# A token encoder with linear attention and routed experts: normalising undivided heads, copying the doubled payload columns on ScalarE, and moving one down product and one image's places

## The chip, the cores and the metric

The kernel runs on 1 core of one Trainium2 chip. The metric is the device time of one execution in microseconds; lower is better. The engines are TensorE (PE, matmuls), VectorE (DVE), ScalarE (ACT), GpSimd (POOL) and the DMA queues, among them SyncE's (SP). Each engine takes its own instructions strictly in the order in which they were written, and waits on semaphores for the others.

## The reference

Four images of 512 tokens, model width 192. Every token first gets a Fourier feature projection; then one layer of gated linear attention and one layer of routed and shared experts follow, each with a residual. Cut to what matters here:

```python
h = einsum('bnf,of->bno', concat([sin(xb), cos(xb)]), W)      # xb = 2*pi*x*freq, 6912 features
h = concat([cls_tok, h], axis=1)
# attention, x = layernorm(h)
numerator   = einsum('blm,blmd->bld', q, Mstate)
denominator = einsum('blm,blm->bl', q, z)[..., None] + 1e-06
heads  = numerator / denominator
normed = (heads - mean(heads)) / sqrt(var(heads) + 1e-05) * gamma + beta
h = h + normed @ Wo
# experts, x = layernorm(h)
top-2 of 8 experts by softmax(x @ router_w), gates normalised to sum 1
routed = sum_e gate_e * (silu(x @ w_gate_e) * (x @ w_up_e)) @ w_down_e
shared = (silu(x @ ws_gate) * (x @ ws_up)) @ ws_down
h = h + alpha * shared + (1 - alpha) * routed                   # alpha = sigmoid(x @ sg_w + sg_b)
```

## The kernel before

The order of every engine's work is written out by hand. Attention runs for five sequences a: a = 0 is the class token (2 rows, the same for all images), a = 1 to 4 (B = 4) are the images with four tiles of 128 tokens. The program has three stretches.

**Token stretch.** For each image b, `project(b, k)` for k = 0 to 8 multiplies the sine and cosine features of nine blocks (L1369, 48 matmul instructions a block as the profile counts them). The features come from POOL (L426), DVE (`remainders`, L801 and L805) and ACT (`sines`, L511 and L514). The attention of the image before is woven between the blocks on every engine: `attn0(a)` ... `attn8(a)`. For a = 0 this runs inside image 0's own nine blocks.

**Shared stretch.** After the last block, PE runs 24 chunks q (6 for each image) of the shared expert: `up(q)` (two products of five matmuls, L1533 to L1537), with `down(q - 2)` (L1571) behind it. ACT makes `silu(q)` (L616), DVE `hidden(q)` (L1077). `up(q)` waits for `hidden(q - 2)`, `down(q)` for `hidden(q)`, and the first `down` of an image waits for `finish` of the image before (L1085, semaphore `out_ready`), which empties its PSUM banks. 19 chunks (NQB) run here, and the attention of image 4 (a = B) is woven in by a table of chunk numbers: `Q_LN2` = 6 (its heads), `Q_X2` = 7, `Q_LN3` = 9 (third layernorm), `Q_X3` = 10 (transposes), `Q_LG` = 11, `Q_RK` = 12 (router, gates, ranks).

**Tile stretch.** Tokens are scattered by expert into `slots` in HBM, from two copies of the payload (`pay_a`, `pay_b`), by POOL's indirect DMAs (L456), which wait for the positions that `places(a, [1])` writes (L1053). SP then loads `xs` from `slots` (L386) in groups of 1, 2, 4, 5, ... tiles, and 39 tiles run through `tile_x`, `tile_up`, `tile_hidden_t` and `tile_down`. The last five shared chunks and the combination follow.

Steps that the change touches:

- `attn5(a)` on DVE: `divide` adds 1e-6 to the denominators (L900), takes reciprocals (L904) and writes the divided heads from PSUM into `xn` (L908); `norm_heads` then runs `layernorm` on `xn`: bn_stats (L771), bn_aggr (L774), twelve steps of Newton's inverse square root on four numbers a row (L778 to L784), and the final subtract and multiply (L787).
- `layernorm(..., twice=True)` in `attn7(a)`: the payload has 256 columns, of which the last 64 repeat columns 128 to 192 (for the high and low parts of a product). DVE writes them with an instruction of its own for each tile (L790). PE's `attn8(a)` transposes columns 0 to 128 (L1491) and 128 to 256 (L1493); POOL's `second_payload` copies the payload (L441).
- `places(B, ...)`: three pieces of small DVE steps that turn ranks into positions.
- `down(NQB - 1)`: the down product of chunk 18, the first of image 4, in the tile loop; it waits for `finish(2)`, which DVE runs behind `tile_low(0)`.

## Time and profile before

| | us |
|---|---|
| median of 3 runs | 556.94 |
| lowest, highest | 554.76, 557.33 |
| the profiled execution's own time | 554.62 |
| its span, first to last instruction | 552.8 |
| PE busy in it | 535.8 |
| DVE busy | 370.3 |
| ACT busy | 244.4 |
| POOL busy | 180.3 |

The span is cut by what PE does: about 6 to 350 us is the token stretch, 352 to 443 us the shared stretch, 443 to 525 us the tiles, and the rest is the tail. The granted TensorE clock is full in all slices.

A row of the timeline reads: start in us from the span's start, length in us, engine, line, operation, output <- inputs, shape, number of merged instructions, and in brackets the engine's idle time before it with what ended it. A matmul's end is modelled: in a dense row of 0.40 us matmuls the next one starts 0.23 us after the one before, so an idle time understates the delay against a dense follower by about 0.15 us.

### The profile page before, as it was taken

What the parts mean: (1) busy time and instruction counts of PE and PEld (TensorE: products, weight loads), DVE (VectorE), ACT (ScalarE), POOL (GpSimd) and SP (SyncE); (2) the same over time, 40 slices, a digit from 0 to 9 for tenths busy, and PEclk for the clock granted to TensorE, in tenths of its full rate; (3) what the DMA queues carried; (4) which work ended last, traced back from release to release, by engine and by line L of the source; (5) the groups of instructions that cost most, each with busy time, mean ns of one, the idle gap of its engine ahead of it and who ended that gap; (6) DMA issues with size and microseconds to landing.
All of it is one profiled execution on the core that took longest, in us unless ns stands there. A gap on an engine that the chain in (4) does not pass through costs nothing.

```text
span 552.8 us, 9034 instructions
## 1 busy us (share of the span) xinstructions
PE 535.8 (97%) x3235; PEld 504.8 (91%) x3235; DVE 370.3 (67%) x1065; ACT 244.4 (44%) x343; POOL 180.3 (33%) x205
## 2 busy tenths in 40 slices
PE   5999999999999999999999999999999999999997
PEld 5998999899999899999989999978877899999865
DVE  8637787534868637978853995468998256666437
ACT  3465464755324764243565422264142135555410
POOL 6413134122234311765212460002601414444510
PEclk9999999999999999999999999999999999999999
DMA  8900067000000001110000010510103441531174
GB/s 330 341 23 20 7 219 250 20 10 20 20 19 21 20 0 27 62 59 0 1 1 10 20 59 1 185 54 30 50 0 125 157 136 47 171 99 51 52 216 142
DMA packets 23488, 42.49 MB, mean 77 GB/s; under 512 B 2502, under 2 KB 15044, under 8 KB 23348
## 3 DMA queue, kind: packets, MB, share of 16 engines
q1 hardware_dynamic: 19560, 33.31, 18.4%
q0 software_dynamic: 3472, 8.07, 4.1%
q10 hardware_dynamic: 412, 0.53, 0.4%
q8 instruction: 27, 0.44, 0.3%
q14 instruction: 17, 0.14, 0.1%
HBM read 31.74 MB, written 14.79 MB: 84 GB/s over the span
## 4 chain that ended last, share of the span: by engine, by line
PE 80%; DVE 11%; ACT 4%; issue 2%; DMA 1%; ACTq 0%; DVEq 0%
PE ps L1369 44%; PE ps L1571 3%; PE ps L1624 2%; PE ps L1626 2%; PE ps L1533 1%; PE ps L1602 1%; PE ps L1603 1%; PE ps L1604 1%; PE ps L1606 1%; PE ps L1605 1%; DMA r<-r 1%; PE ps L1537 1%; PE ps L1535 1%; PE ps L1536 1%; PE ps L1534 1%
## 5 line engine op out<-in xcount | busy, mean ns | idle before, releaser
L1369 PE MATMUL ps<-w_tok,feat 128*128 128x192 f32 x1728 | 289.4, 328 | 7.5 <-ACT feat L502 6.2
L1369 PEld LDWEIGHTS ps<-w_tok,feat 128*128 128x128 f32 x1728 | 282.9, 191 | 8.7 <-issue 8.7
L426 POOL TENSOR_SCALAR feat<-fx 128x512 int32<-128x512 f32 x108 | 93.4, 880 | 189.4 <-PE ps L1369 185.8
L511 ACT ACTIVATE feat<-feat 128x1536 f32<-128x1536 f32 x35 | 52.0, 1485 | 110.1 <-DVE feat L805 110.1
L801 DVE SCALAR_TENSOR_TENSOR feat<-fx,feat 128x512 f32<-128x512 f32 x105 | 76.5, 781 | 1.8 <-POOL feat L426 1.5
L462 POOL DMA_INDIRECT ydram<-yr,xs x39 | 37.8, 969 | 53.9 <-DVE yr L1127 53.9
L514 ACT ACTIVATE feat<-feat,half_pi 128x1536 f32<-128x1536 f32 x35 | 54.6, 1561 | 0.0
L456 POOL DMA_INDIRECT slots<-pay_a,posi x17 | 17.4, 1025 | 75.2 <-DVE posi L1053 71.8
L805 DVE TENSOR_SCALAR feat<-feat 128x1536 int32<-128x1536 int32 x35 | 37.3, 1066 | 1.2
L1571 PE MATMUL ps<-w_down,hid_ring 128*128 128x192 f32 x192 | 35.4, 328 | 2.2 <-DVE H L1085 2.2
L616 ACT ACTIVATE s_ring<-ps 128x512 f32<-128x512 f32 x24 | 14.4, 599 | 52.4 <-PE ps L1537 52.4
L1571 PEld LDWEIGHTS ps<-w_down,hid_ring 128*128 128x128 f32 x192 | 31.6, 190 | 4.1 <-issue 3.1
L1077 DVE TENSOR_TENSOR hid_ring<-s_ring,ps 128x512 f32<-128x512 f32 x24 | 16.3, 684 | 18.3 <-PE ps L1537 15.3
L638 ACT ACTIVATE xhr<-ps 128x256 fp32r<-128x256 f32 x39 | 15.0, 384 | 22.1 <-PE ps L1584 22.1
L1120 DVE TENSOR_TENSOR hidt<-sr,ps 128x192 f32<-128x192 f32 x39 | 13.8, 354 | 15.8 <-ACT sr L644 15.8
L1113 DVE TENSOR_TENSOR xlr<-ps,xhr 128x256 fp32r<-128x256 f32 x39 | 16.5, 424 | 10.6 <-ACT xhr L638 10.6
L1533 PE MATMUL ps<-X,wa_hi 128*128 128x512 f32 x48 | 22.0, 458 | 0.8 <-ACT s_ring L616 0.8
L849 DVE TENSOR_TENSOR_SCAN r<-one,s_c,r 128x512 f32<-128x512 f32 x4 | 5.1, 1283 | 25.4 <-ACT r L556 25.4
L1127 DVE TENSOR_SCALAR yr<-ps,xs 128x192 f32<-128x192 f32 x39 | 16.3, 418 | 8.6 <-PE ps L1626 8.6
L644 ACT ACTIVATE sr<-ps 128x192 f32<-128x192 f32 x39 | 12.9, 330 | 20.1 <-PE ps L1606 20.1
L456 POOL DMA_INDIRECT slots<-pay_b,posi x17 | 19.0, 1120 | 5.2 <-issue 5.2
L1624 PE MATMUL ps<-wd_ea,htr 128*128 x78 | 19.2, 328 | 0.7 <-DVE yr L1127 0.7
(306 smaller groups left out, 859.6 us busy)
## 6 DMA issues: line engine op xcount, KB each, us to landing
slots<-in_blank SPq DMA_DIRECT2D x1, 5031.0 KB, 19.2
w_tok<-in_wT SPq DMA_DIRECT2D x7, 576.0 KB, 8.9
fx<-in_xT SPq DMA_DIRECT2D x15, 256.0 KB, 2.7
xs<-slots SPq DMA_DIRECT2D x5, 645.0 KB, 5.8
yin<-ydram SPq DMA_DIRECT2D x8, 384.0 KB, 6.6
raw_a<-in_wea SPq DMA_DIRECT2D x4, 384.0 KB, 5.4
raw_b<-in_web SPq DMA_DIRECT2D x4, 384.0 KB, 6.0
w_tok<-in_wT SPq DMA_DIRECT2D x4, 288.0 KB, 7.5
```

Of the source, the lines that this page charges most:

```text
L426: ins = pool.tensor_scalar(feat[:, k % SLOTS, i, :].bitcast(I32), x[:, x_block(k), :], f_col[:, fi:fi + 1], 1.0, ALU.mult, ALU.mult)
L456: pool.indirect_dma_start(slots, bass.IndirectOffsetOnAxis(ap=idx, axis=0), (pay_a[a % 2], pay_b)[c][0:TP, t, :], None).then_inc(scat, 16)
L462: pool.indirect_dma_start(ydram, bass.IndirectOffsetOnAxis(ap=idx, axis=0), yr[:, s % NYR, :], None).then_inc(yscat[s % NYR], 16)
L511: act.activation(feat[:, k % SLOTS, 0:3, :], feat[:, k % SLOTS, 0:3, :], ACT.Sin, scale=TWO_PI).then_inc(sin_ready, 1)
L514: act.activation(feat[:, k % SLOTS, 3:6, :], feat[:, k % SLOTS, 3:6, :], ACT.Sin, bias=half_pi[:, :], scale=-TWO_PI).then_inc(sin_ready, 1)
L801: ins = dve.scalar_tensor_tensor(feat[:, s, i, :], x[:, x_block(k), :], f_col[:, fi:fi + 1], feat[:, s, i, :].bitcast(I32), ALU.mult, ALU. ...
L805: dve.tensor_scalar(feat[:, s, 3:6, :].bitcast(I32), feat[:, s, 0:3, :].bitcast(I32), 0x7FFFFFFF, None, ALU.bitwise_and).then_inc(r_ready, 1)
L1113: dve.tensor_tensor(xlr[:, s % 2, :], ps[:, XT[s % 2], 0:2 * P], xhr[:, s % 2, :].bitcast(F32), ALU.subtract).then_inc(rxl_ready, 1)
L1369: ins = pe.matmul(ps[:, TOK[a % 2][t // 2], (t % 2) * D:(t % 2 + 1) * D], feat[:, k % SLOTS, i, t * P:(t + 1) * P], w_tok[:, k, i, :], sta ...
L1533: pe.matmul(o, wa_hi[:, c, i, :], xh, start=True, stop=False)
L1571: ins = pe.matmul(ps[:, DN0 + t // 2, (t % 2) * D:(t % 2 + 1) * D], hid_ring[:, q % 3, t * P:(t + 1) * P], w_down[:, c, :], start=(c == 0 ...
L1624: pe.matmul(o, htr[:, s % 2, 0:P], wd_ea[:, bass.ds(e, 1), :].rearrange("p e n -> p (e n)"), start=True, stop=False)
```

## The change

1. **Heads.** The reciprocal and the divided copy are gone. With h = s/d (d is the denominator plus 1e-6), (h - mean h) / sqrt(var h + eps) equals (s - mean s) / sqrt(var s + eps d^2) for positive d, so `layernorm` now reads the undivided sums s in PSUM, and its variance gets eps d^2 (`den2`) in place of eps. DVE's bn_stats and its last step both read PSUM.
2. **Doubled columns.** L790 is gone for all five sequences. ACT copies columns 128 to 192 to 192 to 256 in one instruction, `twice(a)`, which waits for `xn2_ready` and raises `twice_ready`. PE's second group of transposes and POOL's `second_payload` wait for `twice_ready`. For a = 0 to 3 `twice` stands ahead of ACT's `attn8(a)`, for a = 4 ahead of `silu(10)`.
3. **Places of image 4.** `places(B, [0])` goes from before to after `hidden(12)`, `places(B, [1])` from after `hidden(12)` to after `hidden(14)`.
4. **Last chunk's down product.** `down(18)` goes from the tile loop's turn 1 to turn 2, behind `tile_hidden_t(0)`.

```diff
@@ DVE, layernorm
-            def layernorm(src, dst, a, which, TP, nt, done, twice=False, parts=(0, 1, 2)):
+            def layernorm(src, dst, a, which, TP, nt, done, over=None, parts=(0, 1, 2)):
...
                     for i in range(nt):
-                        ins = dve.bn_stats(st[0:TP, i, :], src[0:TP, i, 0:D])
+                        ins = dve.bn_stats(st[0:TP, i, :], src(i))
+                    if over is not None:
+                        for lo, d in over:
+                            n = d.shape[1]
+                            ins = dve.tensor_scalar(den[0:TP, lo:lo + n], d, DEN_EPS, None, ALU.add)
                     next_(ins)
                     for i in range(nt):
                         ins = dve.bn_aggr(mv[0:TP, i, :], st[0:TP, i, :])
+                    if over is not None:
+                        ins = dve.scalar_tensor_tensor(den2[0:TP, 0:nt], den[0:TP, 0:nt], LN_EPS, den[0:TP, 0:nt],
+                                                       ALU.mult, ALU.mult)
...
-                    next_(dve.tensor_scalar(v_, mv[0:TP, 0:nt, 1], LN_EPS, None, ALU.add))
+                    if over is None:
+                        next_(dve.tensor_scalar(v_, mv[0:TP, 0:nt, 1], LN_EPS, None, ALU.add))
+                    else:
+                        next_(dve.tensor_tensor(v_, mv[0:TP, 0:nt, 1], den2[0:TP, 0:nt], ALU.add))
...
-                        if twice:
-                            ins = dve.tensor_scalar(dst[0:TP, i, D:XD], src[0:TP, i, P:D], mv[0:TP, i, 0:1],
-                                                    y[0:TP, i:i + 1], ALU.subtract, ALU.mult)
@@ DVE, attn5
-            def divide(a):
...
-                dve.reciprocal(rden[0:TP, 0:nt], den[0:TP, 0:nt]).then_inc(rden_ready, 1)
...
-                    ins = dve.tensor_scalar(xn_[0:TP, i, 0:D], ps[0:TP, AV_BANK[i // 2], c0:c0 + D],
-                                            rden[0:TP, i:i + 1], None, ALU.mult)
...
+                layernorm(heads, normed(a), a, 1, TP, nt, hn_ready, over=sums)
@@ ACT
+            def twice(a):
+
+                act.wait_ge(xn2_ready, a + 1)
+                act.activation(payload(a)[:, :, D:XD], payload(a)[:, :, P:D], ACT.Copy).then_inc(twice_ready, 1)
+
             def attn8(a):
...
+                if a < B:
+                    twice(a)
                 act.wait_ge(xpose3, a + 1)
...
+                if q == Q_X3:
+                    twice(B)
                 silu(q)
@@ POOL, second_payload
-                pool.wait_ge(xn2_ready, a + 1)
+                pool.wait_ge(twice_ready, a + 1)
@@ DVE, main order
                     gates(B)
-                    places(B, [0])
...
                 hidden(q)
...
                 if q == Q_RK:
+                    places(B, [0])
+                if q == Q_RK + 2:
                     places(B, [1])
-                if q == Q_RK + 2:
                     places(B, [2])
@@ PE, attn8
+                pe.wait_ge(twice_ready, a + 1)
                 for i in range(nt):
                     ins = pe.transpose(ps[:, A1, i * P:(i + 1) * P], pay_[:, i, P:XD], ident)
@@ PE, tile loop
-                if i == 1:
-                    down(NQB - 1)
                 if 2 <= i < NTILE + 2:
                     tile_hidden_t(i - 2)
+                if i == 2:
+                    down(NQB - 1)
```

PE's order at the end of the class token's attention (a = 0, between blocks 6 and 7 of image 0), before:

```order
L1369 MATMUL ps<-w_tok,feat 128x192 x11
L1369 MATMUL ps<-w_tok,feat 128x192 [waits sin_ready]
L1369 MATMUL ps<-w_tok,feat 128x192 x11
L1491 MATMUL ps<-pack,pay_a 128x128 [waits xn2_ready]
L1493 MATMUL ps<-pack,pay_a 128x128
L1369 MATMUL ps<-w_tok,feat 128x192 [waits sin_ready,wt_in7]
```

and with the change:

```order
L1374 MATMUL ps<-w_tok,feat 128x192 x11
L1496 MATMUL ps<-pack,pay_a 128x128 [waits xn2_ready]
L1499 MATMUL ps<-pack,pay_a 128x128 [waits twice_ready]
L1374 MATMUL ps<-w_tok,feat 128x192 [waits sin_ready,wt_in7]
L1374 MATMUL ps<-w_tok,feat 128x192 x11
```

Nothing moved, but the second transpose got a wait. What that wait is for stands on ACT; its order at the same place with the change (L511 and L514 are `sines(0, 7)`, L593 is `twice(0)`, L603 and L604 `attn8(0)`):

```order
L511 ACTIVATE feat<-feat 128x1536 [waits r_ready]
L514 ACTIVATE feat<-feat,half_pi 128x1536
L593 ACTIVATE pay_a<-pay_a 2x64 [waits xn2_ready]
L603 ACTIVATE xc<-ps 128x2 [waits xpose3]
L604 ACTIVATE xc<-ps 128x2
L511 ACTIVATE feat<-feat 128x1536 [waits r_ready]
```

The copy is new, and stands behind both sine instructions of block 7.

DVE's order over chunks 12 to 14, before (L1030 to L1041 are `places(B, [0])`, L1043 to L1055 `places(B, [1])`, L1059 begins `places(B, [2])`):

```order
L1011 TENSOR_TENSOR pay_b<-p,om 128x4
L1030 TENSOR_TENSOR aft<-cnt,rks 128x8 [waits rk_ready]
...
L1041 SCALAR_TENSOR_TENSOR dd<-gap,dold 128x8 [waits pos_step]
L1077 TENSOR_TENSOR hid_ring<-s_ring,ps 128x512 [waits silu_ready,down_ready,u_psum,pos_step]
L1043 TENSOR_TENSOR slot<-rks,base 128x32
...
L1053 CAST posi<-posf 128x8 [waits scat,pos_step]
L1055 COPY cnt<-aft 128x8
L1077 TENSOR_TENSOR hid_ring<-s_ring,ps 128x512 [waits silu_ready,down_ready,u_psum,pos_step]
L1085 SCALAR_TENSOR_TENSOR H<-ps,alpha,H 128x192 [waits down_ready]
L1085 SCALAR_TENSOR_TENSOR H<-ps,alpha,H 128x192 x3
L1077 TENSOR_TENSOR hid_ring<-s_ring,ps 128x512 [waits down_ready,silu_ready,u_psum]
L1059 COPY nbk<-nba 128x8
```

and with the change:

```order
L1017 TENSOR_TENSOR pay_b<-p,om 128x4
L1083 TENSOR_TENSOR hid_ring<-s_ring,ps 128x512 [waits down_ready,silu_ready,u_psum]
L1036 TENSOR_TENSOR aft<-cnt,rks 128x8 [waits rk_ready]
...
L1047 SCALAR_TENSOR_TENSOR dd<-gap,dold 128x8 [waits pos_step]
L1083 TENSOR_TENSOR hid_ring<-s_ring,ps 128x512 [waits silu_ready,down_ready,u_psum,pos_step]
L1091 SCALAR_TENSOR_TENSOR H<-ps,alpha,H 128x192 [waits down_ready]
L1091 SCALAR_TENSOR_TENSOR H<-ps,alpha,H 128x192 x3
L1083 TENSOR_TENSOR hid_ring<-s_ring,ps 128x512 [waits down_ready,silu_ready,u_psum]
L1049 TENSOR_TENSOR slot<-rks,base 128x32
...
L1059 CAST posi<-posf 128x8 [waits scat,pos_step]
L1061 COPY cnt<-aft 128x8
L1065 COPY nbk<-nba 128x8 [waits pos_step]
```

`finish(1)` (L1085, now L1091) now stands ahead of the piece that writes the positions `posi`.

## Rows read from the trace of the kernel before

**Rows 1.** The page: busy time (us), share of the span, instructions, by engine.

```profile
PE 535.8 (97%) x3235; PEld 504.8 (91%) x3235; DVE 370.3 (67%) x1065; ACT 244.4 (44%) x343; POOL 180.3 (33%) x205
```

**Rows 2.** Waits of PE: line <- what it waited for: us in total, times, longest.

```profile
PE ps L1571 <- DVE H L1085: 2.2, 3, 1.1
```

**Rows 3.** Timeline of PE at the class token's last transposes.

```profile
68.73 0.27 PE L1493 MATMUL ps<-pack,pay_a 128*128 128x128 f32 x1
69.20 8.04 PE L1369 MATMUL ps<-w_tok,feat 128*128 128x192 f32 x48 [0.20 <-ACT feat L511]
```

**Rows 4.** Timeline of ACT there.

```profile
67.56 1.49 ACT L511 ACTIVATE feat<-feat 128x1536 f32<-128x1536 f32 x1 [6.57 <-DVE feat L805]
68.95 1.56 ACT L514 ACTIVATE feat<-feat,half_pi 128x1536 f32<-128x1536 f32 x1
70.42 0.15 ACT L596 ACTIVATE xc<-ps 128x2 fp32r<-128x2 f32 x1
```

**Rows 5.** Timeline of ACT at the same place of image 3.

```profile
342.62 0.60 ACT L596 ACTIVATE X<-ps 128x512 fp32r<-128x512 f32 x1 [7.88 <-PE ps L1493]
```

**Rows 6.** Timeline of DVE, heads of image 4 and what follows.

```profile
384.35 1.39 DVE L908 TENSOR_SCALAR xn<-ps,rden 128x192 f32<-128x192 f32 x4
...
394.03 3.69 DVE L1106 TENSOR_TENSOR e_b<-raw_b,e_b 64x384 fp32r<-64x384 f32 x2
```

**Rows 7.** Timeline of POOL there.

```profile
391.96 4.86 POOL L477 TENSOR_TENSOR e_lo<-raw_a,e_hi 128x384 fp32r<-128x384 f32 x5
```

**Rows 8.** Timeline of PE, shared stretch.

```profile
391.34 0.66 PE L1466 MATMUL ps<-pack,xn 128*128 128x128 f32 x4 [0.55 <-DVE xn L787]
...
399.29 1.54 PE L1571 MATMUL ps<-w_down,hid_ring 128*128 128x192 f32 x8 [0.61 <-DVE H L1085]
...
407.58 0.66 PE L1491 MATMUL ps<-pack,pay_a 128*128 128x128 f32 x4 [0.80 <-DVE pay_a L790]
...
412.36 0.24 PE L1505 MATMUL ps<-wra_hi,X 128*128 128x10 f32 x1
```

**Rows 9.** Timeline of DVE at the end of the third layernorm of image 4.

```profile
407.22 0.31 DVE L790 TENSOR_SCALAR pay_a<-H,mv,y 128x64 f32<-128x64 f32 x1
407.44 1.28 DVE L1077 TENSOR_TENSOR hid_ring<-s_ring,ps 128x512 f32<-128x512 f32 x2
```

**Rows 10.** Timeline of ACT: `silu(10)` and `silu(12)`.

```profile
405.65 0.60 ACT L616 ACTIVATE s_ring<-ps 128x512 f32<-128x512 f32 x1 [2.21 <-PE ps L1537]
...
419.91 0.60 ACT L616 ACTIVATE s_ring<-ps 128x512 f32<-128x512 f32 x1
```

**Rows 11.** Timeline of DVE: places of image 4 around `hidden(12)`.

```profile
420.64 0.17 DVE L1030 TENSOR_TENSOR aft<-cnt,rks 128x8 f32<-128x8 f32 x1 [0.97 <-ACT rks L609]
...
422.68 0.69 DVE L1077 TENSOR_TENSOR hid_ring<-s_ring,ps 128x512 f32<-128x512 f32 x1
423.29 0.18 DVE L1043 TENSOR_TENSOR slot<-rks,base 128x32 f32<-128x32 f32 x1
```

**Rows 12.** Timeline of PE: end of `up(14)`, then `down(12)`.

```profile
425.62 0.40 PE L1537 MATMUL ps<-X,wb 128*128 128x512 f32 x1
427.11 1.54 PE L1571 MATMUL ps<-w_down,hid_ring 128*128 128x192 f32 x8 [1.10 <-DVE H L1085]
```

**Rows 13.** Timeline of POOL: the first scatter of image 4.

```profile
425.66 1.00 POOL L456 DMA_INDIRECT slots<-pay_a,posi  x1 [16.77 <-DVE posi L1053]
```

**Rows 14.** Timeline of SP's queue: the first six loads of `xs`.

```profile
437.16 3.02 SPq L386 DMA_DIRECT2D xs<-slots  x6
```

**Rows 15.** DMA issues: count, KB each, median us to landing; here the first tile.

```profile
xs<-slots SPq DMA_DIRECT2D x1, 129.0 KB, 2.0
```

**Rows 16.** Timeline of PE: first tile, and `down(18)`.

```profile
443.00 0.27 PE L1583 MATMUL ps<-pack,xs 128*128 128x128 f32 x1
...
446.26 1.54 PE L1571 MATMUL ps<-w_down,hid_ring 128*128 128x192 f32 x8 [0.47 <-DVE H L1085]
```

**Rows 17.** Timeline of DVE in the first tiles: `tile_low(1)`, right behind `finish(2)`.

```profile
446.03 0.41 DVE L1113 TENSOR_TENSOR xlr<-ps,xhr 128x256 fp32r<-128x256 f32 x1
```

44 lines of the change are left out of this document (17 added, 27 removed).

## The prediction

> **What bounds the kernel now.** I read the page's busy table first: PE is busy 97% of the span, DVE 67%, ACT 44% [rows 1]. Work saved on DVE or ACT is worth nothing in itself. It counts only where PE waits, so the next view is PE's waits. The largest class in the part that the change touches is PE waiting for `finish` in front of a `down`, 2.2 us in three waits [rows 2]. Then I went through PE's timeline for every idle time in brackets, and asked of each what the waited-for engine had been doing. Outside the first 7 us and the tail, the waits within reach of the change are 0.55 us before the transposes of the heads, 0.61 before `down(6)`, 0.80 before the payload's transposes [rows 8], 1.10 before `down(12)` [rows 12] and 0.47 before `down(18)` [rows 16], all on DVE and all in the shared stretch or just behind it. In the token stretch PE has nearly no wait to give back, so there the change can only cost: what has to be looked for is a wait that it adds on a PE that is dense. Times below are positions in the old trace, and gains or losses are of PE against it.
>
> **1. The class token's `twice(0)`: a loss of 1.4 us.** PE's second transpose for a = 0 ran at 68.73, and block 7 followed at 69.20 after 0.20 us of idleness, when `sines(0, 7)` had finished its first half [rows 3]. Now that transpose waits for `twice(0)`, and `twice(0)` stands on ACT behind both halves of `sines(0, 7)`. These started at 67.56 and 68.95, and the next instruction, `attn8(0)`, started at 70.42 [rows 4]. Queued behind the waiting transpose is all of PE's block 7. One L790 less on DVE ahead of it brings the sines forward by its pitch, 407.44 - 407.22 = 0.22 us [rows 9]: `twice(0)` starts at 70.20. The trace has no ACT copy of 2x64; it lasts at least the 0.15 us of the 128x2 copy in [rows 4], and at most the 0.60 of a 128x512 [rows 5]; I take 0.24, near the small one. Then 0.04 for the semaphore, transpose at 70.48, block 7 some 0.12 later at 70.60, against 69.20: **+1.40**, between +1.3 and +1.75. From there PE is dense to image 4 and everything else in the token stretch follows PE, so nothing gives it back.
>
> For a = 1 to 3 the same wait costs nothing. ACT had sat idle for 7.88 us before image 3's `attn8` [rows 5] and longer in image 1, so it takes the copy as soon as DVE is done, while PE is still in block 7. The shorter heads and layernorms on DVE in these images are hidden under the blocks.
>
> **2. Heads of image 4: gained, then given back, 0.** The removed copy took 1.39 us [rows 6], the reciprocal and its wait some 0.2 more. Against that stand `den2`, two small operations that now share a group with others, and bn_stats from PSUM instead of SBUF. No row has bn_stats from PSUM; its bounds are its present 1.14 for four and the 1.39 that the copy from PSUM took for four, so at most 0.25 more. DVE is done at least 1.2 us sooner. PE was late by 0.55 plus the 0.15 of a modelled end, 0.7 us, so this wait goes. But DVE's next long step is not its own: L1106 (`expert_lo(0)` and `(1)`) started at 394.03 and the pair took 3.69 us, though POOL's e_lo subtractions ran to 391.96 + 4.86 = 396.82 and DVE only came through behind them [rows 6, 7]. POOL began those when its scatter of image 3 was out, which the change doesn't move. So DVE reaches L1106 at about 393.3 and leaves it at 397.7 as before; `finish(0)` and PE's `down(6)` at 399.29 stay where they are, and the wait there grows from 0.61 to about 1.3. Net **0**.
>
> The Trainium skill (SBUF — State Buffer, "SBUF: two separate sides") says that the port pair is locked for one instruction, by whichever engine starts first. By that, DVE would get in at the first boundary between POOL's five, near 393.9, and not behind the fifth; the trace of before speaks against it, since DVE came at 394.03 and passed two such boundaries unserved. What the rule would give is rival B.
>
> **3. Payload of image 4: 0.4 us.** Without four L790, less the one pitch each that they took (4 x 0.22), the last layernorm ends at 406.63 instead of 407.53, so the transposes start 0.90 sooner. `twice(4)` on ACT moves half of the 128x512 that took 0.60 [rows 5], so I take 0.4 of it; the first four transposes take 0.66 less their modelled end [rows 8], 0.5: no wait of PE, or 0.1 if the copy takes the full 0.60. But `twice(4)` stands ahead of `silu(10)`, which ran at 405.65 [rows 10] and now cannot start before 406.63 + 0.05 + 0.3 = 407.0 (0.3 being the pitch of such a copy, 0.1 under its length). Queued behind is `hidden(10)`: DVE could do it at 407.15 and gets it at 407.63, where it was at 408.04. Of the 0.90, DVE keeps 0.41. The rest of DVE's row (three `expert_lo`, the low parts of the operand) runs without a pause to PE's router at 412.36 [rows 8]. PE arrives 0.90 early and waits for DVE there: **-0.41** in all.
>
> **4. Places after `hidden(12)`: 1.3 us.** Today `places(4, [0])` starts at 420.64, `hidden(12)` at 422.68, `places(4, [1])` at 423.29 [rows 11], then `hidden(13)`, then `finish(1)`, for which PE waits 1.10 + 0.15 = 1.26 us behind the end of `up(14)` (425.62 + 0.23 = 425.85 against 427.11) [rows 12]. With the new order `hidden(12)` goes as soon as `silu(12)` is there: 419.91 + 0.60 - 0.41 = 420.10 [rows 10]. Piece 0 takes 422.68 - 420.64 = 2.04 and starts one pitch of 0.6 later, at 420.73, so `hidden(13)` stands at 422.77 and `finish(1)` runs 423.37 to 424.76. PE comes to `down(12)` at 425.85 - 0.41 - 0.04 = 425.40 and finds it done. **-1.30**; PE is now 1.71 ahead.
>
> **5. The scatter is late: 0.85 us given back.** Piece 1, which releases POOL's scatter, now stands behind `finish(1)` and `hidden(14)`. The latter needs `up(14)`: in a dense row it starts 0.44 after PE's last matmul, so 425.62 - 0.45 + 0.44 = 425.61, and piece 1 at 426.22, where it was at 423.29 [rows 11]: 2.93 us later. POOL's eight scatters, then SP's loads, then the first tile move by that: POOL 425.66 to 428.59 [rows 13], SP 437.16 to 440.09 [rows 14], landing 2.0 later [rows 15], 442.09. PE would take the first tile at 443.00 - 1.71 = 441.29 [rows 16]. It waits to about 442.15: **+0.85**. Before, the tile had landed 3.8 us ahead. The bounds are 0 (if the landing is 0.85 shorter) and 1.5 (landing at the 2.7 of the second load). Later groups have more slack, since a tile takes PE some 2 us.
>
> **6. `down(18)` a turn later: 0.** The 0.47 + 0.15 us before it [rows 16] goes. But DVE still runs `finish(2)` ahead of `tile_low(1)`, which starts 3.03 us after PE's first tile and ends at 3.44 [rows 17], and `tile_up(1)` needs it. `down(18)` covered that; without it PE arrives at 2.80 and waits 0.65. Turn 3 begins 5.98 after turn 0, against 5.95. **+0.03**, within 0.3 either way.
>
> **Sum:** 1.40 + 0 - 0.41 - 1.30 + 0.85 + 0.03 = +0.57 us. On the profiled execution's 554.62 that is 555.2. That execution lies at the low end of the three runs, 2.3 us under their median, so for the median I add it to 556.94: **557.5**. About 0.5% (2.8 us) is what a measurement of this kernel can tell from no change.
>
> **Rivals.**
> A, the steps as above, 557.5: chance 0.66.
> B, DVE slips in between POOL's subtractions: `finish(0)` would run some 2 us sooner, and PE would keep 0.7 + 0.6 + 0.9 + 0.2 = 2.4 us to the router, then 1.3 at `down(12)`; the first tile, whose scatter follows PE there, takes back about 0.8. With +1.4 from step 1 that is -1.5: 555.4. The passed boundaries speak against it. 0.08.
> C, the first tile comes in time after all, or the class token's wait is shorter than the queue says (ACT free sooner): -0.3 to -0.8, 556.4. Nothing in the rows shows a shorter landing; 0.10.
> D, slower: `twice(4)` on ACT costs DVE all that it saved, because `silu(10)` comes later than 407.3, and the places' new turn then does not free `finish(1)` in time while the scatter is late all the same. PE has +1.4, neither gain, and waits at the first tile 0.4 to 1.5 us for a landing 2.9 to 4 us late: +1.8 to +3, 559.3. It decides from the point where `hidden(12)` is more than 1 us later than I place it. Against it: `silu(12)` has no other work ahead of it than before. 0.09.
> E, that it does not do what it says: PE's doubled transposes for images 1 to 3 wait too, because `twice` stands behind `sines(b, 8)`. That costs up to 1.4 us an image, +4.8: 561.7. ACT's idle 7.88 us speaks plainly against it. 0.02. The remaining 0.05 is for medians of three that fall apart more than the steps: those before differ by 2.6 us.
>
> **Range.** The likeliest case with the bounds of steps 1, 5 and 6 spans 556.5 to 558.8; the spread of a median and cases B, C and part of D widen it to 555.0 to 559.6. Faster by over 0.5% (below 554.2) needs B and more: 0.04. Slower by over 0.5% (above 559.7) is half of D, and E: 0.07. Within: 0.89.
>
> **What the profile would show.** Step 1: PE idle about 1.5 us before the class token's second transpose, with ACT's small copy as its releaser, right behind L514. Step 2: no wait before the heads' transposes, a wait of about 1.3 before `down(6)`, and again one DVE instruction of some 3 to 4 us beside POOL's e_lo. Step 3: `silu(10)` right behind the copy, PE waiting 0.5 before the router. Step 4: no wait before `down(12)`. Step 5: PE waiting for a DMA before the first tile. Step 6: the wait before `down(18)` gone and one of 0.5 to 0.7 before the second tile's up product. I am wrong if PE shows no wait for the class token's copy, or if the first tile starts dense.

## The result, and the profile after

| | before | after |
|---|---|---|
| median, us | 556.98 (11 runs) | 560.05 (11 runs) |
| lowest, highest | 554.46, 557.52 | 557.33, 560.34 |
| ratio after to before, 95% interval | | 1.0053 [1.0032, 1.0075] |
| profiled execution: own time, span | 554.62, 552.8 | 560.13, 558.3 |
| mean granted TensorE clock in it | 1.000 | 0.993 |

The changed kernel is 3.1 us slower. The forecast was 557.5 with a range up to 559.6, so the result lies outside. Eight more runs of the same kernel on another chip gave 560.11 (ratio 1.0073 [1.0048, 1.0097]).

The first thing to see stands in the last row of the table: the two profiled executions did not have the same clock. Their spans differ by 5.5 us, their kernels' medians by 3.1.

**PE's waits.** In the view of PE's waits after the change (what waited, for whom, us in total, times, longest), the row of [rows 2] has shrunk from 2.2 to 1.4, and five rows are new or larger:

```profile
PE ps L1499 <- ACT pay_a L593: 1.6, 1, 1.6
PE ps L1577 <- DVE H L1091: 1.4, 1, 1.4
...
PE ps L1589 <- DMA xs<-slots: 1.0, 1, 1.0
...
PE ps L1608 <- DVE xlr L1119: 0.7, 1, 0.7
...
PE ps L1511 <- issue: 0.5, 1, 0.5
PE ps L1577 <- issue: 0.5, 1, 0.5
```

**Class token.** ACT's timeline: both sines, and right behind them the new copy. It answers to [rows 4], where the row at 70.42 followed the sines directly:

```profile
67.85 1.48 ACT L511 ACTIVATE feat<-feat 128x1536 f32<-128x1536 f32 x1 [6.35 <-DVE feat L825]
69.24 1.56 ACT L514 ACTIVATE feat<-feat,half_pi 128x1536 f32<-128x1536 f32 x1
70.70 0.24 ACT L593 ACTIVATE pay_a<-pay_a 2x64 f32<-2x64 f32 x1
```

PE's timeline in the same place, against 68.73 and 69.20 in [rows 3]:

```profile
71.00 0.33 PE L1499 MATMUL ps<-pack,pay_a 128*128 128x128 f32 x1 [1.58 <-ACT pay_a L593]
71.16 0.34 PE L1374 MATMUL ps<-w_tok,feat 128*128 128x192 f32 x1
```

Block 7 starts 1.96 later, and from its third matmul on the difference is 1.90. PE was already 0.52 late ahead of it, so this place costs 1.38. The 0.52 is from the first 12 us, where the kernels are the same: PE's matmuls there start 0.32 us apart at first and 0.16 apart later, and the step from one to the other comes at about 10.7 us before and 11.6 us after. In the other profiles of this document this early difference against before lies between -0.5 and +0.8 us, whatever the kernel.

**Heads, `down(6)`, `down(12)`, first tile.** PE's timeline at the places of [rows 8], [rows 12] and [rows 16]. The wait before the heads' transposes (395.75) is gone, the one before `down(6)` has grown from 0.61 to 1.40, the payload's (411.82) is gone, the router (417.12) waits 0.54, `down(12)` (430.62) waits no more, and three waits stand in the first tile turns, 0.97, 0.47 and 0.70:

```profile
395.75 0.49 PE L1471 MATMUL ps<-pack,xn 128*128 128x128 f32 x3
...
404.41 0.56 PE L1577 MATMUL ps<-w_down,hid_ring 128*128 128x192 f32 x2 [1.40 <-DVE H L1091]
...
411.82 0.66 PE L1496 MATMUL ps<-pack,pay_a 128*128 128x128 f32 x4
...
417.12 0.24 PE L1511 MATMUL ps<-wra_hi,X 128*128 128x10 f32 x1 [0.54 <-issue]
...
430.62 0.65 PE L1577 MATMUL ps<-w_down,hid_ring 128*128 128x192 f32 x3
...
447.56 0.30 PE L1589 MATMUL ps<-pack,xs 128*128 128x128 f32 x1 [0.97 <-DMA xs<-slots]
447.70 0.27 PE L1590 MATMUL ps<-pack,xs 128*128 128x128 f32 x1
448.44 0.42 PE L1577 MATMUL ps<-w_down,hid_ring 128*128 128x192 f32 x1 [0.47 <-issue]
...
452.02 0.44 PE L1608 MATMUL ps<-e_hi,xhr 128*128 x1 [0.70 <-DVE xlr L1119]
...
454.51 0.27 PE L1589 MATMUL ps<-pack,xs 128*128 128x128 f32 x1
```

The first tile (447.56) now waits for its landing, where before it started dense at 443.00 [rows 16].

**The clock.** The view by windows gives, for each stretch, the busy time and instruction count of PE, PEld, DVE, ACT and POOL, then the granted clock. Two stretches of 3.4 us in the middle of dense work ran at 0.50, that is at 1.2 GHz instead of 2.4:

```profile
182.00:185.60 3.60, 3.60 (x33) 3.60 (x31) 2.82 (x7) 2.05 (x2) 2.74 (x3) 1.00 0.00 0
185.70:189.00 3.30, 3.30 (x13) 3.30 (x12) 2.99 (x14) 3.25 (x5) 0.00 (x0) 0.50 0.00 0
...
353.60:356.30 2.70, 2.70 (x25) 2.66 (x24) 1.34 (x7) 2.16 (x3) 0.00 (x0) 1.00 0.48 113
356.40:359.70 3.30, 3.30 (x10) 2.53 (x9) 2.85 (x17) 0.60 (x1) 0.00 (x0) 0.50 0.96 299
```

PE was busy without a gap ahead of either (3.60 of 3.60 us and 2.70 of 2.70). What it did there was the row of 20 small router matmuls of an image (10 columns each): image 1's ahead of the first stretch, image 3's ahead of the second. PE's timeline shows the end of such a row and then the shared expert's products, which stand 0.43 us apart where they are 0.23 apart at full clock:

```profile
355.86 0.25 PE L1515 MATMUL ps<-wrb,X 128*128 128x10 f32 x1
355.97 0.48 PE L1539 MATMUL ps<-X,wa_hi 128*128 128x512 f32 x1
...
357.51 0.63 PE L1543 MATMUL ps<-X,wb 128*128 128x512 f32 x1
357.94 0.63 PE L1539 MATMUL ps<-X,wa_hi 128*128 128x512 f32 x1
```

PE's starts against those of before move by 1.68 us over the first stretch and by 1.55 over the second. So the 5.5 us between the two spans are 0.5 from the start, 3.2 from two half-clock stretches and 1.8 from waits. The forecast had 0.57 for the waits and nothing for the clock.

### The profile page after: what moved, and what is told of

Same layout as the page of the kernel before. It is cut to its first block, busy times and chain, and to the rows that moved or that the text cites. A ratio compares the mean times of both kernels' runs of the same rounds, so it can differ in the third digit from the quotient of the medians.

```text
span 558.3 us, 9004 instructions
## 1 busy us (share of the span) xinstructions
PE 539.3 (97%) x3235; PEld 508.0 (91%) x3235; DVE 361.9 (65%) x1031; ACT 246.0 (44%) x348; POOL 176.4 (32%) x205
## 4 chain that ended last, share of the span: by engine, by line
PE 82%; DVE 7%; ACT 4%; issue 2%; DMA 2%; POOL 1%; ACTq 0%; DVEq 0%; POOLq 0%
PE ps L1374 44%; PE ps L1577 3%; PE ps L1630 2%; PE ps L1632 2%; PE ps L1539 2%; PE ps L1541 1%; PE ps L1542 1%; PE ps L1540 1%; PE ps L1543 1%; PE ps L1608 1%; POOL slots L456 1%; PE ps L1610 1%; PE ps L1609 1%; PE ps L1612 1%; PE ps L1611 1%
## 5 line engine op out<-in xcount | busy, mean ns | idle before, releaser
L426 POOL TENSOR_SCALAR feat<-fx 128x512 int32<-128x512 f32 x108 | 88.4, 833 | 196.1 <-PE ps L1374 192.3
L511 ACT ACTIVATE feat<-feat 128x1536 f32<-128x1536 f32 x35 | 51.9, 1484 | 104.8 <-DVE feat L825 104.7
L514 ACT ACTIVATE feat<-feat,half_pi 128x1536 f32<-128x1536 f32 x35 | 54.6, 1561 | 0.0
```

What stands on the lines that cost most here:

```text
L426: ins = pool.tensor_scalar(feat[:, k % SLOTS, i, :].bitcast(I32), x[:, x_block(k), :], f_col[:, fi:fi + 1], 1.0, ALU.mult, ALU.mult)
L511: act.activation(feat[:, k % SLOTS, 0:3, :], feat[:, k % SLOTS, 0:3, :], ACT.Sin, scale=TWO_PI).then_inc(sin_ready, 1)
L514: act.activation(feat[:, k % SLOTS, 3:6, :], feat[:, k % SLOTS, 3:6, :], ACT.Sin, bias=half_pi[:, :], scale=-TWO_PI).then_inc(sin_ready, 1)
```

## The experiments

Every run's mean granted clock is listed with its time, and the times of one kernel fall into groups by it. The kernel before, in 112 runs beside these experiments: 48 runs at 1.0 of 554.4 to 555.3, 64 below it of 556.7 to 560.6. "Full-clock runs" below are those at 1.0. Because the share of them differs from kernel to kernel, a median mixes waits and clock; the full-clock runs and the trace tell the waits apart. The diffs show the lines that decide; declarations of semaphores and waits that only follow from them are left out.

**1. The changed kernel with the class token's columns back on DVE**, written by `layernorm` for a = 0 again.

```diff
@@ ACT, attn8
-                if a < B:
+                if 0 < a < B:
                     twice(a)
@@ PE, attn8
-                pe.wait_ge(twice_ready, a + 1)
+                if a >= 1:
+                    pe.wait_ge(twice_ready, a)
```

> The changed kernel, with the class token's doubled columns written by VectorE again (its ScalarE copy and TensorE's wait for it gone); all else as changed. Theory W (waits): TensorE loses 1.40 us at this wait, and nothing later gives it back, so this kernel is 1.4 us faster than the changed one, 1.0 to 1.8, near 558.6, and its trace has no wait at the class token's second transpose. Rival C (clock): most of the 3 us comes from stretches at half the TensorE clock that the changed kernel's 1.6 us stall brings on; then the stall's removal takes those stretches away too, in profile and times, and the gain is 2.5 us or more. Rival H (hidden): the next stages are not paced by TensorE and absorb it, gain under 0.5 us.

Measured: 558.05 (555.0 to 561.36, 12 runs), ratio 1.0030 [1.0010, 1.0050]. The profiled execution was at full clock, with a span of 553.2 against 552.8 before, and PE's shift is -0.04 up to `down(6)`, -0.93 at the payload, -0.41 at the router, -1.67 at `down(12)`, -0.57 at the first tile, +0.10 behind it and +0.43 at turn 3. So the class token's copy accounts for the whole 1.38, and the rest of the change costs 0.4 us instead of gaining the 0.83 of the forecast. The two full-clock runs (mean 555.07, before 554.95) give 0.1. Two of 12 runs were at full clock, so taking the wait away did not bring the clock back.

**2. The class token's copy alone**, on the kernel before, and again on another chip.

```diff
@@ ACT, attn8
+                if a == 0:
+                    twice(0)
@@ DVE, layernorm
-                        if twice:
+                        if twice and a != 0:
@@ PE, attn8
+                if a == 0:
+                    pe.wait_ge(twice_ready, 1)
```

> The kernel before, with only the class token's doubled columns copied by ScalarE behind both sine halves of block 7. Theory W: +1.4 us against before in every run of like clock, 1.2 to 1.7; a wait of 1.6 us at the second transpose, everything behind it shifted by the same. Rival C: the stall adds half-clock stretches, so the share of runs with them rises and the median rises by 2.5 us or more. Rival H: under 0.5 us.

> The kernel before with the class token's copy on ScalarE alone, again, on the same chip as the others of this call. Theory W: 1.4 us over before at like clock, with a third to a half of the runs at full clock. Rival C: none at full clock, and the runs with one stretch have it between 60 and 80 us, behind the stall of 1.6 us, where no other kernel has one.

Measured: 560.13 (557.24 to 560.35, 12 runs), ratio 1.0046 [1.0027, 1.0065]; again 557.85 (556.96 to 560.45, 12 runs), ratio 1.0049 [1.0027, 1.0071]. This one small copy makes the kernel nearly as slow as the whole change, with a wait of 1.59 in the trace (1.6 in the view of waits) and PE 1.38 later behind it. No run of the 24 was at full clock. The profile of the first has three half-clock stretches, the second's has one. The second's, by windows: the router row, then the stretch.

```profile
181.80:183.80 2.00, 2.00 (x22) 2.00 (x19) 1.87 (x2) 0.78 (x1) 2.00 (x3) 1.00 0.00 0
184.80:188.10 3.30, 3.30 (x12) 3.30 (x11) 2.96 (x15) 3.25 (x5) 0.00 (x0) 0.50 0.00 0
```

The first stretch behind the wait at 70 us begins more than 110 us later, but within 1 us of the end of a router row. That speaks against a direct effect of the wait.

The expectation of 1.4 us "in every run of like clock" was not met. At a mean clock of 0.997 the four runs of the first set are 0.5 us over those of before beside them, at 0.994 the three are 2.8 over. A mean clock says how much of the run was at half clock, not behind which row, and it does not see the early difference of up to 0.8 us.

The copy alone also costs a second, smaller time, which none of the other kernels has. In the shared stretch, ahead of the table load for `silu`, ACT sits idle for 1.65 us in all three profiles that have the copy alone (these two and that of experiment 8), and 1.37 in all others. ACT's timeline, copy alone with the routers spread (experiment 8), then before:

```profile
375.77 1.28 ACT L625 ACT_TABLE_LOAD   x1 [1.65 <-DVE r L869]
```
```profile
371.70 1.28 ACT L616 ACT_TABLE_LOAD   x1 [1.37 <-DVE r L860]
```

PE waits 1.03 us there instead of 0.75, and stays 0.28 later. So by the traces this kernel's waits cost 1.38 + 0.28 = 1.66 us. DVE, which the row names, was done as early as before; why ACT starts later is not shown.

**3. The places alone.**

```diff
@@ DVE, main order
                     gates(B)
-                    places(B, [0])
...
                 if q == Q_RK:
+                    places(B, [0])
+                if q == Q_RK + 2:
                     places(B, [1])
-                if q == Q_RK + 2:
                     places(B, [2])
```

> The kernel before, with only the two pieces of image 4's places moved. Theory W: the wait before down(12) goes (-1.26), hidden(12) and finish(1) come some 2 us sooner; POOL's scatter starts later by 2.9 us, the first tile's data lands near 3 us later than now, and TensorE waits there. Without the 0.4 us from the other edits TensorE arrives at 441.7 on the old scale and waits about 0.5 plus the 0.7 that it took behind that wait in the changed kernel before the next product: net 0 to -0.3 us. Rival P (places pay): if the slow expert read behind the wait is of something else, the net is -0.8 or better.

Measured: 557.66 (555.36 to 558.33, 10 runs), ratio 1.0015 [0.9999, 1.0032]. In the trace `down(12)` gives 1.25, the first tile takes 1.05 back, and then another 0.66 goes where I had nothing, in the `down` behind the first tile. PE's timeline:

```profile
445.54 0.30 PE L1583 MATMUL ps<-pack,xs 128*128 128x128 f32 x1 [0.96 <-DMA xs<-slots]
...
446.43 0.75 PE L1571 MATMUL ps<-w_down,hid_ring 128*128 128x192 f32 x3 [0.47 <-issue]
```

The move of the places is by itself a loss of 0.5 us (-1.25 + 1.05 + 0.66). Its one full-clock run (555.36 against 554.95) says 0.4. The profile has two half-clock stretches, at 272.4 and 354.4, in a kernel whose first 400 us are those of before: they come without any wait of the class token.

**4. The expert number read ahead of the first tile.** PE reads the tile's expert number into a register between `tile_x(i)` and the `down` behind it. In the dense row of before that read cost nothing that shows (443.10 to 443.21). My guess for the 0.66 was that behind a wait it is exposed. Here it is read once ahead of the loop.

```diff
@@ PE, tile loop (changed kernel)
-            expert = {}
+            expert = {0: pe.value_load(emapi[0:1, 0:1], min_val=0, max_val=NE - 1)}
             for i in range(NTILE + 3):
                 if i < NTILE:
                     tile_x(i)
+                if 0 < i < NTILE:
                     expert[i] = pe.value_load(...)
```

> The changed kernel, with the expert number of tile 0 read from emapi before the first tile's transposes instead of behind them. In the changed kernel TensorE sat idle 0.97 us for the data and then 0.47 more between the transposes and down(17). Theory R (read exposed): the second idle time is TensorE's sequencer reading the number from memory with nothing queued ahead; read before the wait it is hidden under down(16) or the wait for data, so the idle time before down(17) goes and the tiles start 0.5 to 0.7 us sooner. Rival S: it is the wait for hidden(17) or the cost of any first matmul behind a DMA wait; then nothing changes, within 0.2 us in the trace.

Measured: 560.21 (559.46 to 560.71, 5 runs), ratio 1.0065 [1.0041, 1.0089]: no gain that the times can show. In the trace:

```profile
447.55 0.33 PE L1589 MATMUL ps<-pack,xs 128*128 128x128 f32 x1 [1.03 <-DMA xs<-slots]
447.71 0.27 PE L1590 MATMUL ps<-pack,xs 128*128 128x128 f32 x1
447.82 1.47 PE L1577 MATMUL ps<-w_down,hid_ring 128*128 128x192 f32 x8
...
450.33 0.44 PE L1608 MATMUL ps<-e_hi,xhr 128*128 x1 [0.54 <-ACT xhr L645]
...
451.47 0.43 PE L1608 MATMUL ps<-e_hi,xhr 128*128 x1
```

The down product follows the tile at once, at 447.82 and not at 448.44. A new wait of 0.54 comes in the first up product, the one of 0.70 in the second goes, and that second up product starts at 451.47 instead of 452.02. So the read was the cause of the 0.47 wait. In the traces, PE is 0.5 us less late at the end of the tiles than in the changed kernel, early differences taken off.

**5. The heads alone**, on the kernel before.

```diff
@@ DVE, attn5
-                dve.reciprocal(rden[0:TP, 0:nt], den[0:TP, 0:nt]).then_inc(rden_ready, 1)
...
+                layernorm(heads, normed(a), a, 1, TP, nt, hn_ready, over=sums)
```

> The kernel before with the heads normalised from undivided sums, and nothing else of the change. My steps: PE's 0.55 us wait before the heads' transposes goes, the wait before down(6) grows from 0.61 to 1.3, net 0 within 0.2 at full granted clock (554.7 where the kernel before has 554.7). Rival, DVE slips in between POOL's subtractions: 0.6 to 1.4 us faster. On router rows and half-clock stretches: no row moves by more than 0.2 us, so the share of runs at full clock should be like that of the kernel before (39 of 87 so far), where the kernels with the class token's wait show none in 48.

Measured: 557.27 (555.05 to 557.65, 10 runs), ratio 1.0018 [0.9999, 1.0037]. DVE's timeline behind the heads, where [rows 6] had the pair in 3.69, and PE's `down(6)`:

```profile
395.60 4.44 DVE L1111 TENSOR_TENSOR e_b<-raw_b,e_b 64x384 fp32r<-64x384 f32 x2
400.06 0.42 DVE L1090 SCALAR_TENSOR_TENSOR H<-ps,alpha,H 128x192 f32<-128x192 f32 x1
```
```profile
401.61 0.56 PE L1575 MATMUL ps<-w_down,hid_ring 128*128 128x192 f32 x2 [1.38 <-DVE H L1090]
```

PE gained 0.72 at the heads and lost 0.70 up to `down(6)`: DVE came to its `expert_lo` pair 0.8 us sooner and left it no sooner, so the pair grew by 0.75. The full-clock runs (555.10, two of them, against 554.67) do not show a gain either.

**6. The same heads, with `expert_lo` out of the way**: its first two pieces come one chunk later, behind `finish(0)`. If the gain of the heads was lost to POOL's five subtractions, it has to appear now.

```diff
@@ constants (heads alone, as in 5)
-Q_LO = (7, 7, 8, 10, 10, 10, 11, 11)
+Q_LO = (8, 8, 8, 10, 10, 10, 11, 11)
```

> The kernel before with the undivided heads alone, and with VectorE's expert_lo(0) and (1) moved from before finish(0) to behind hidden(8). Theory L (the gain at the heads is lost to the shared port): in the changed kernel VectorE's first such instruction took as long as GpSimd's row of five subtractions lasted, and finish(0) stood behind it. With finish(0) first, down(6) does not wait (under 0.2 us, 1.1 to 1.4 in the changed kernel), the three expert_lo still wait for the end of the row or run after it, and TensorE comes to the payload's transposes ahead: 1.5 to 3 us under before at like clock. Rival: VectorE is short of time anyway, and the wait moves to the payload's transposes, gain under 0.5 us.

Measured: 553.09 (552.69 to 555.58, 10 runs), ratio 0.9963 [0.9943, 0.9983]. The wait before `down(6)` is gone. PE starts it 0.99 earlier than before and is 1.56 ahead at the payload, though this execution was 0.57 late ahead of the heads: the gain is 1.56 at `down(6)` and 2.13 at the payload. DVE's and POOL's timelines side by side:

```profile
393.72 1.39 DVE L1090 SCALAR_TENSOR_TENSOR H<-ps,alpha,H 128x192 f32<-128x192 f32 x4
395.90 0.69 DVE L1082 TENSOR_TENSOR hid_ring<-s_ring,ps 128x512 f32<-128x512 f32 x1 [0.79 <-PE ps L1541]
396.62 2.13 DVE L1111 TENSOR_TENSOR e_b<-raw_b,e_b 64x384 fp32r<-64x384 f32 x3
```
```profile
392.54 4.85 POOL L477 TENSOR_TENSOR e_lo<-raw_a,e_hi 128x384 fp32r<-128x384 f32 x5
```

POOL's row runs from 392.54 to 397.39. `finish(0)` and `hidden`, which read one operand from PSUM, go through it at their usual 1.39 and 0.69. The pair with both operands in SBUF, which was held in experiment 5, now comes when POOL is nearly through, and three of its kind take 2.13 us. So the gain was there and had been lost behind the held pair: against where it stood ahead of the heads, PE is level at `down(6)` without the changed number (0.02 early) and 1.56 early with it. Only one of the ten runs was at full clock (553.08). The six at 0.996 or 0.997 took 552.69 to 553.16, so in this kernel the time at half clock cost little; none of them was profiled.

**7. `down(18)` alone**, one turn later, on the kernel before.

```diff
@@ PE, tile loop
-                if i == 1:
-                    down(NQB - 1)
                 if 2 <= i < NTILE + 2:
                     tile_hidden_t(i - 2)
+                if i == 2:
+                    down(NQB - 1)
```

> The kernel before with down(18) moved one turn back in the tile loop, and nothing else. My step 6 says 0 to +0.3 us at full granted clock: the 0.47 us wait before down(18) goes, and one of 0.5 to 0.7 before the second tile's up product takes its place. What the trace of the changed kernel left open is whether its +0.34 there came from this move or from the late first tile; here the first tile is early, so +0.0 speaks for the late tile and +0.3 for the move. Clock: the router rows stand as before, so the share of runs at full clock should be like that of the kernel before.

Measured: 555.11 (554.69 to 557.57, 10 runs), ratio 0.9995 [0.9974, 1.0016]. The 0.47 before it has gone, and the wait of the second up product is there with an early first tile too:

```profile
446.95 0.44 PE L1602 MATMUL ps<-e_hi,xhr 128*128 x1 [0.69 <-DVE xlr L1113]
...
449.45 0.27 PE L1583 MATMUL ps<-pack,xs 128*128 128x128 f32 x1
```

Turn 3 starts 0.50 later than before, where PE was 0.24 late ahead of the tiles: the move costs 0.26, and its eight full-clock runs (555.03 against 554.67) say 0.36. Eight of 10 were at full clock; the median (555.11 against 556.91 of before beside it) looks like a gain for that reason alone.

**8. Router rows spread out.** If the small matmuls bring the half-clock stretches, mixing them into the projection has to remove these. For images 1 to 3 the five router matmuls of each tile are now set apart from the next tile's by a sixth of a block (8 large matmuls): in block 1 of the next image for images 1 and 2, in the last block of the token stretch for image 3. The row of image 4 stays. Three kernels have it: before, changed, and before with the class token's copy alone.

```diff
@@ PE, main order
-                    router(b - 1)
-                project(b, 1)
+                    for i in range(NT):
+                        router(b - 1, (i,))
+                        project(b, 1, (i,) if i < NT - 1 else range(NT - 1, 6))
...
-            router(B - 1)
+            project(B - 1, 8, range(3))
+            for i in range(3):
+                router(B - 1, (i,))
+                project(B - 1, 8, (3 + i,))
+            router(B - 1, (3,))
```

> The kernel before, with the 20 small router matmuls (10 columns each) of images 1 to 3 no longer in one row on TensorE: each tile's five stand between groups of 8 large matmuls of a block. Image 4's router stays. In every trace so far that has a stretch of 3.4 us at half the TensorE clock inside the kernel, it began 0.7 to 3 us after such a router row ended. Theory R (router rows bring the half clock): with the rows spread, the half-clock stretches behind images 1 to 3 go, most runs have a mean granted clock of 0.997 or more, and the median falls from 557.0 to about 555, at most 555.8. Rival F (they come at set times or at random): the share of runs at 0.994 stays near a half and the median within 0.5 us of before.

> The changed kernel with the same spread of the router matmuls of images 1 to 3. Of the 3.07 us between the medians, the traces give 1.9 to one-off waits (by runs at full clock, which the changed kernel has none of). Theory R: the rows' stretches go here too, the median falls from 560.05 to 557 to 558, and is 1.9 to 2.5 us over the spread kernel before. Whether any run is at full clock tells about the class token's 1.6 us stall: if that stall brings a half-clock stretch of its own in some runs, there remain runs at 0.997 beyond those that image 4's router explains. Rival F: median within 0.5 us of 560.05.

> The kernel before with the class token's doubled columns copied by ScalarE, and with the router matmuls of images 1 to 3 laid between the projection's blocks instead of in one row of 20. Beside it stands the same spread without the copy (556.59 us in its runs at full granted clock). Waits alone: the class token's wait is 1.4 us in the trace and PE stays that much late, so the runs at full clock lie at 556.6 + 1.4 = 558.0, and about half of the runs or more are at full clock, since nothing but a router row brings a half-clock stretch. Rival, the class token's stall brings a half-clock stretch by itself: hardly a run at full clock, median above 559.5, and the profile shows a stretch with no router row within 2 us ahead of it.

| routers spread | median, us (range, runs) | at full clock | mean of those |
|---|---|---|---|
| before | 557.62 (556.38 to 558.11, 12) | 5 of 12 | 556.59 |
| class token's copy alone | 558.68 (558.35 to 559.4, 10) | 7 of 10 | 558.86 |
| changed | 558.5 (558.02 to 562.67, 9) | 5 of 9 | 558.39 |

Ratios to the kernel before: 1.0029 [1.0013, 1.0046], 1.0040 [1.0023, 1.0057] and 1.0071 [1.0043, 1.0100]. The spread itself costs 1.9 us (556.59 against 554.67 to 554.95 at full clock), but among themselves the three compare directly. Changed minus before, both at full clock, is 1.8 us, as the waits in the trace of the changed kernel (1.82); the profiled pair of these two, 2.0 apart with 0.5 of it from the first 12 us, gives 1.5. And with the class token's wait in place, 7 of 10 runs and 5 of 9 stay at full clock (a sixth run had 0.999), where without the spread it was none of 24 and none of 24 (19 of the changed kernel, 5 with the early read). By windows the profile of the copy alone is at 1.00 from 12 to 550 us:

```profile
12.00:180.00 168.00, 165.01 (x1016) 160.19 (x1015) 111.78 (x295) 83.23 (x79) 50.51 (x61) 1.00 0.26 84
180.00:360.00 180.00, 178.31 (x1116) 172.65 (x1114) 124.29 (x370) 82.04 (x79) 64.84 (x69) 1.00 0.09 28
360.00:550.00 190.00, 183.86 (x1069) 163.34 (x1070) 122.11 (x363) 73.73 (x179) 59.51 (x63) 1.00 0.30 99
```

So the wait does not bring a stretch by itself. The copy alone stands 2.27 above before and not 1.4. In the profiled pair it is 2.1, of which 0.48 was there at 12 us, ahead of anything changed, 1.38 at the class token, and 0.28 at the table load of experiment 2, which the whole change does not have. That is also part of the 0.5 by which the full-clock runs of the whole change lie below those of the copy alone; the rest I cannot place.

Two things speak against the simple form of theory R. The kernel before was to fall to about 555 and got slower instead, 557.62, and its share of runs at full clock did not rise (5 of 12, against 16 of 32 for the unspread kernel beside it). And three of the nine changed runs had a mean clock of 0.994 and took 562.3 to 562.7, 4 us over the others. A mean of 0.994 over their 560.8 us is about 6.7 us at half clock, where in the profiles the one row left, image 4's, brings 3.4 at most and the end of the kernel 1.3. None of the three was profiled. So spreading helps the kernels with the class token's wait, and router rows may not be all that brings half clock.

**9. The changed kernel again**, on another chip, for a second look at where the half clock falls.

> The changed kernel again, unaltered, beside the kernel before on one chip: how are its runs spread over the granted clocks? Theory W says that at full clock it would be 1.9 us over before at full clock, 556.6 to 556.9, and that a like share of runs (a third to a half) is at full clock. Rival C (the class token's stall brings half-clock stretches): no run at full clock again, as in the first 11, and the median stays 3 us over before.

Measured: 560.11 (557.34 to 561.18, 8 runs). The profiled execution is that of 557.34: the same waits (1.58, 1.11, 0.56, 0.94, 0.48, 0.70), and only one half-clock stretch before the tail. The router row of image 1 brought none this time, that of image 3, the last before the shared stretch, did:

```profile
350.90:352.90 2.00, 2.00 (x20) 2.00 (x18) 0.66 (x3) 1.55 (x3) 0.00 (x0) 1.00 0.35 34
354.40:357.70 3.30, 3.30 (x10) 2.53 (x9) 2.95 (x15) 0.60 (x1) 0.00 (x0) 0.50 1.03 362
181.00:184.00 3.00, 3.00 (x29) 3.00 (x27) 2.33 (x4) 1.45 (x2) 2.73 (x3) 1.00 0.00 0
```

The same rows of the same kernel bring a stretch in one execution and not in the next. What the two traces show to differ ahead of the row of image 1 is its time: this execution was 0.49 early behind the first 12 us where the other was 0.52 late. These 1.0 us and the stretch's 1.7 make up nearly all of the 2.8 between 557.34 and 560.13.

Over all twelve profiles with the rows in one piece, the row of image 1 sorts by its start. In eight it begins between 180.0 and 181.4 us, and none has a stretch behind it; in four it begins between 181.9 and 182.6, and all four have one. Those four all have the class token's wait, and the one profile that has the wait and an early row, this one, has no stretch there. The row of image 3 does not sort as cleanly: it brought a stretch where it began at 351.0 (this one), and none at 353.2 (the second profile of experiment 2).

**10. A version that beats both.** The changed kernel with what the runs had shown: the class token's columns on DVE, `expert_lo` a chunk later, `down(18)` back, and `places(B, [1])` right behind `finish(1)`, ahead of `hidden(14)`, so that the scatter does not wait for `up(14)`. Once as such and once with the routers spread.

```diff
@@ DVE, main order
                     finish(q // NCS - 1)
+                if q == Q_RK + 2:
+                    places(B, [1])
                 hidden(q)
```

> The candidate without the spread of the router rows. The spread kernel before showed in its trace at full clock what the spread costs: 1.8 us of new waits (0.6 at the scores of images 2 and 3, 1.0 at image 4's first transposes). Theory W: without it the candidate at full clock is 1.6 to 1.9 us under the spread one, near 551.6, that is 3.1 us under before at full clock; the shares of half-clock runs go back to those of before, so the median is 552.5 to 554. Rival: the half-clock stretches behind the router rows cost more than the spread, and the median is no better than 553.4.

> A version meant to beat both: the changed kernel with the class token's doubled columns on VectorE, piece 1 of image 4's places directly behind finish(1) and ahead of hidden(14), down(18) back in turn 1, VectorE's expert_lo(0) and (1) behind finish(0) and hidden(8) instead of in front of them, and the router rows spread. Theory W: no wait for the class token; VectorE does not stand in front of GpSimd's five subtractions while finish(0) is due, so down(6) waits under 0.3 us and the 0.7 gained at the heads is kept; scatter some 1.5 us later than before, first tile in time: 2.5 to 3.5 us under the kernel before in a trace at full clock, near 552.0. With theory R also fewer half-clock stretches: median 551.5 to 553. Rival L: VectorE is blocked later by the same subtractions, and the gain stays with the router spread and the places, 553.5 to 555.

Measured: without the spread 553.43 (553.0 to 556.46, 12 runs), ratio 0.9967 [0.9943, 0.9992]; with it 553.4 (552.88 to 555.83, 12 runs), ratio 0.9968 [0.9951, 0.9985]. PE's waits in the first, behind the two of the start, are down to:

```profile
PE ps L1544 <- ACT s_ring L623: 0.8, 1, 0.8
PE ps L1635 <- DVE yr L1136: 0.7, 1, 0.7
...
PE ps L1582 <- DVE H L1094: 0.5, 1, 0.5
```

Both beat the kernel before by 0.3% and the changed one by over 1%. They can't be told from experiment 6, which needs only the heads and one number. The 551.6 that was expected without the spread at full clock was never seen: none of its 12 runs was at full clock, though it has no wait of the class token. The profiled one (553.22, mean clock 0.996) has its only stretch before the tail behind image 4's row, at 413.7 to 417.0, and PE is 1.6 us later for it. With the spread, the four full-clock runs took 552.94.

## Why the prediction was wrong, point by point

| step | forecast | trace after | alone |
|---|---|---|---|
| 1 class token | +1.40 | +1.38 | +1.38 (2, 8) |
| 2 heads, `down(6)` | 0 | 0.00 | -0.02 (5) |
| 3 payload, router | -0.41 | -0.36 | |
| 4 `down(12)` | -1.30 | -1.25 | -1.25 (3) |
| 5 first tile | +0.85 | +1.05 | +1.05 (3) |
| the `down` behind it | not in the sum | +0.67 | +0.66 (3) |
| 6 `down(18)` | +0.03 | +0.33 | +0.26 (7) |
| sum of waits | +0.57 | +1.82 | |
| half-clock stretches | not in the sum | +3.2 in this execution | |

(The measured figures are differences of PE's start against before at the rows shown, each less the one ahead of it, for step 1 from the third matmul of block 7 on; in the last column the number of the experiment in brackets.)

All six signs that it named for the profile are there, and neither of the two that would have refuted it. So the mechanism of each step held; what failed are the size of step 5, a term behind it that was left out, and the clock.

**Step 1 was right** to 0.02: the copy took the 0.24 that I had taken for it, and sat behind both sines. I had written down the right price for what turned out to be the worst part of the change: the copy alone gives ratios of 1.0046 and 1.0049 (experiment 2), with the clock and the 0.28 at the table load in them.

**Step 2 was right**, and rival B with it refuted. The pair at [rows 6] became 4.44 and 4.46, longer by as much as DVE came sooner. In the trace after, DVE enters at 398.38, while POOL's five run from 397.09 to 401.95, and leaves at 402.84: it passed the three boundaries still ahead of it unserved. The Trainium skill (SBUF — State Buffer, "SBUF: two separate sides") has the pair locked for the whole of one instruction, and a DVE operation with two SBUF inputs among those that need it; the second half agrees with experiment 6, where PSUM operands passed. The first half does not tell the whole here: DVE was out until the end of the row. What I had not seen is that the way out was as near as experiment 6 shows.

**Steps 3 and 4 were right** to 0.05. `silu(10)` stands behind the copy (412.12 behind 411.80), the router waits 0.54.

**Step 5 was mis-sized.** First, the wait for the landing is 1.05 and not 0.85. Shifting my own times by the 5.17 us that PE was later at the router than I had placed it gives SP at 445.26 (measured 445.37) and the landing at 447.32 (447.56): 0.2 too short. Second, and worse, the step ended at the first tile. It named what waits for the tile, and not what is queued behind a PE that has run dry. In the dense row of before, the same read lay between the second transpose (443.10) and the product behind it (443.21), and cost nothing that shows. Behind the wait it stood open, and PE lost 0.67 more (experiments 3 and 4). With these two, the places' move (steps 4 and 5) is a loss of 0.5 where the sum had a gain of 0.45.

**Step 6 was mis-sized** by 0.2 to 0.3, within its own bound. The wait came where it was expected (0.70, forecast 0.5 to 0.7), and with an early tile too, so it belongs to the move.

**The step that was missing is the clock.** The prediction took the granted clock for a constant of the kernel because its row is full in [rows 1]'s page, and carried a sum made on an execution of 554.62 over to a median of 556.94. It noted that the execution stood 2.3 us under that median and did not ask what the others had. Of before no execution below full clock was profiled, but its times group by the clock, 554.8 on average at full and 557.2 below. By its time, the median of three at 556.94 is already a run below full clock. With the waits alone added, the median is 556.98 + 1.8 = 558.8, inside the range. The other 1.3 us of the 3.07 go with the clock: the changed kernel was at full clock in none of 19 runs, before in 48 of 112. That the waits' 1.8 us lie in rival D's bounds is chance: D's reasons, a late `silu(10)` that costs DVE its gain and a `finish(1)` that stays blocked, did not come. And the lower end of the range was added up wrongly: the bounds of steps 1, 5 and 6 reach down to 556.3 and not 556.5, which decides nothing here.

**What is shown and what is open.** Shown: the waits' 1.8 us (at full clock, by experiment 8, and in the trace); that all 14 stretches in the dense part, in eight profiles, come right behind a router row; that spreading the rows brings full-clock runs back with all waits in place. Open: why the kernels with the class token's wait and rows in one piece never get through without a stretch (none of 48 runs), and what lies behind the three runs at 0.994 in experiment 8. A likely reason for the first is argued, not shown: whether a row brings a stretch depends on where it falls in time, and the wait moves the rows of images 1 to 3 by 1.4 us. The row of image 1 fits that (experiment 9), that of image 3 only in part. The kernels without the wait and with these rows in one piece do not settle it. Experiments 1, 3, 5 and 7 had 13 of 42 runs at full clock, not far from 48 of 112, but they go from 1 of 10 to 8 of 10. Experiment 6 and the unspread kernel of experiment 10 had 1 of 22, with a single stretch behind image 4's row in the one such run that was profiled. So a kernel can miss full clock without the class token's wait. No run shifted the rows without the wait, which would be the test.

## What to carry to other kernels

If runs of one kernel fall into groups of times, find out which group the profiled execution is from before a sum is carried over to the median. For every step put behind another queue, price the wait by where that queue stands, and for every wait added on a dense engine also price what that engine prepares right behind it. If a gain on one engine ends at an instruction held up by another, move that instruction first: one number in the order table gave here what the whole change did not.
